# A graph kernel's sixteenth batch split in the hops: two of its tiles by dense products, two by gathered rows, 62 dense tiles in place of 64

## The reference

```
h = max(layernorm(x), 0)
x = x + typed_layer(h)            # gathers by source, sums by destination
h = max(layernorm(x), 0)
norm = deg_inv_sqrt[row] * deg_inv_sqrt[col]
out = h
for _ in range(2):                # the two hops
    h = segment_sum(h[row] * norm[:, None], col)
    out = out + h
x = x + out / 3
```

## Time and profile before

| | us |
|---|---|
| median of three runs | 3703.29 (3702.02 to 3703.51) |
| the profiled execution, its own time | 3704.01 |
| its span, first to last instruction | 3701.4 |
| PE busy | 3148.2 (85%) |
| ACT busy | 2655.3 (72%) |
| POOL busy | 2486.7 (67%) |
| DVE busy | 1789.1 (48%) |

### The profile page before, as it was taken

One profiled execution on the slowest core, in us unless ns is written; L12 is line 12 of the kernel. 1 busy time (PEld: TensorE's weight loads), 2 busy tenths in 40 slices (PEclk: granted clock), 3 DMA queues, 4 the chain that ended last, 5 costly groups with the idle time before them and its releaser, 6 DMA issues. The chain is left out here.

```text
span 3701.4 us, 64279 instructions
## 1 busy us (share of the span) xinstructions
PE 3148.2 (85%) x23900; PEld 2851.4 (77%) x23900; DVE 1789.1 (48%) x4166; ACT 2655.3 (72%) x2895; POOL 2486.7 (67%) x2635
## 2 busy tenths in 40 slices
PE   5658888897888866766667999999997999999998
PEld 2346777776777755544556999999997999999998
DVE  4665555455445568889884223332333222222223
ACT  3436666776667655445446889999996899999997
POOL 2467767777777767777775666666664766666666
PEclk8879989998999976677667999999998999999999
DMA  7453233433333275555556788888889778877876
GB/s 237 150 155 102 80 97 85 120 110 98 91 107 112 79 231 181 170 196 191 187 179 205 223 241 249 239 252 247 251 250 317 235 230 236 236 232 235 235 232 200
DMA packets 444208, 694.30 MB, mean 188 GB/s; under 512 B 62390, under 2 KB 373569, under 8 KB 435699
## 3 DMA queue, kind: packets, MB, share of 16 engines
q1 hardware_dynamic: 343827, 447.82, 37.6%
q0 software_dynamic: 99200, 241.92, 23.7%
q10 hardware_dynamic: 864, 0.39, 0.0%
HBM read 514.92 MB, written 174.97 MB: 186 GB/s over the span
## 5 line engine op out<-in xcount | busy, mean ns | idle before, releaser
L1122 POOL DMA_INDIRECT flat<-typed_table,index x1333 | 1299.7, 975 | 464.8 <-issue 400.2
L1289 ACT CAST strip_ring<-stage 128x1792 fp32r<-128x1792 uint8 x896 | 1495.3, 1688 | 147.3 <-PE wide L1492 125.5
L1492 PE MATMUL wide<-table_parts,strip_ring 128*128 128x256 f32 x12544 | 1543.0, 285 | 40.6 <-ACT strip_ring L1289 32.5
L1492 PEld LDWEIGHTS wide<-table_parts,strip_ring 128*128 128x128 f32 x12544 | 1528.3, 193 | 44.4 <-issue 26.3
L1122 POOL DMA_INDIRECT rows<-hop_table,index x1162 | 1111.5, 957 | 611.1 <-issue 313.8
L1271 ACT CAST stage<-wide 128x392 uint16<-128x392 f32 x1344 | 546.9, 516 | 519.6 <-PE wide L1403 519.5
L1403 PE MATMUL wide<-stage,flat 128*128 128x196 bf16 x2688 | 444.7, 284 | 296.5 <-DVE flat L1890 165.9
L1403 PEld LDWEIGHTS wide<-stage,flat 128*128 128x128 bf16 x2688 | 210.4, 107 | 513.3 <-DVE flat L1890 204.0
L1418 PE MATMUL turned_bank<-typed_ring,table_parts 128*128 128x256 f32 x3920 | 535.5, 296 | 77.2 <-ACT typed_ring L1282 70.4
L1835 DVE SCALAR_TENSOR_TENSOR sums<-sums_bank,in_upper,sums 128x128 f32 (+1 forms) x459 | 160.7, 350 | 871.9 <-PE sums_bank L1367 674.9
L1418 PEld LDWEIGHTS turned_bank<-typed_ring,table_parts 128*128 128x128 f32 x3920 | 506.2, 201 | 97.2 <-issue 58.6
(11 more groups left out here) (183 smaller groups left out, 1419.2 us busy)
## 6 DMA issues: line engine op xcount, KB each, us to landing
stage<-strips SPq DMA_DIRECT2D x896, 224.0 KB, 3.8
strips<-stage SPq DMA_DIRECT2D x64, 1568.0 KB
table_parts<-hop_table SPq DMA_DIRECT2D x28, 896.0 KB, 10.1
flat<-typed_table,index POOLq DMA_INDIRECT x1333
rows<-hop_table,index POOLq DMA_INDIRECT x1162
resid<-xin SPq DMA_DIRECT2D x50, 256.0 KB, 3.6
xin<-resid SPq DMA_DIRECT2D x50, 256.0 KB, 5.1
typed_table<-flat SPq DMA_DIRECT2D x49, 256.0 KB, 2.2
```

The lines of the kernel that those rows point to most:

```text
L1122: pool.indirect_dma_start(out=gathered(k, o % RING, c), out_offset=None, in_=tables[k], in_offset=bass.IndirectOffsetOnAxis(ap=index[:, ch ...
L1289: act.copy(strip_ring[:, number % STRIP_RING], counts_ring[place]).then_inc(strip_cast, 1)
L1492: last = pe.matmul(wide[:, nth % 4, 0:PARTS * P], strip_ring[:, number % STRIP_RING, b - first, :], table_parts[:, b, :, :].rearrange("p n ...
```

## The change

The hops now take 62 tiles by dense products. Of the sixteenth batch (number 15, `MIXED`) tiles 60 and 61 are dense, and tiles 62 and 63 come from gathered rows. A hop's gathered part begins at group 130 in place of 135: 78 groups in place of 73. The dense steps are spread over `hop_groups - 6` = 72 slots, so that six slots behind them have none where four had. Since the window moves on at the cut of batch 15 (slot 6 of a hop) and the batch is finished only in slot 74 or 75, a DVE copy puts the sums of the two gathered tiles aside (`later_part`, in a part of `index` that the hops no longer read). The strips of tiles 62 and 63 aren't built, stored or loaded.

```diff
--- before.py
+++ after.py
@@ -32,7 +32,9 @@
 COUNT_BASE = 256
 CELL_BANKS = 3
 DENSE_BATCHES = 16
-DENSE_TILES = DENSE_BATCHES * NODE_BLOCKS
+DENSE_TILES = 62
+MIXED = DENSE_BATCHES - 1
+MIXED_DENSE = DENSE_TILES - MIXED * NODE_BLOCKS
 PAIR_TILES = 9
 PARTS = 2
 STEP_BLOCKS = 14
@@ -41,7 +43,7 @@
 RELOAD_BLOCKS = 7
 RELOADS_AT_ONCE = 3
 STAGE_WORDS = 10320
-DENSE_SLOTS = 69
+SLOTS_BEHIND_DENSE = 6
 LEAD_TILES = 3
 LEAD_AT_ONCE = 3
 TYPED_BATCHES = 5
@@ -130,6 +132,7 @@
     dense_nodes = DENSE_TILES * P
     first_group = next(g for g in range(groups) if expected(g + 1) + MARGIN >= dense_nodes)
     hop_groups = groups - first_group
+    dense_slots = hop_groups - SLOTS_BEHIND_DENSE
     skipped = closed_before(first_group)
     assert skipped == DENSE_BATCHES - 1
     group_of_close = [next((g for g in range(groups - 1) if closed_before(g + 1) > s), groups - 1) for s in range(total)]
@@ -187,7 +190,7 @@
     def step_end(k, i):
 
         rest = steps_per_hop - lead_steps[k]
-        return lead_steps[k] + min(rest, -(-(i + 1) * rest // DENSE_SLOTS))
+        return lead_steps[k] + min(rest, -(-(i + 1) * rest // dense_slots))
 
     def slot_of_step(k, step):
         return next(i for i in range(hop_groups) if step_end(k, i) > step)
@@ -209,7 +212,7 @@
         return placed
 
     def hop_wanted(k):
-        dense = [(tile_slot[k][(s + 1) * NODE_BLOCKS - 1], s) for s in range(DENSE_BATCHES)]
+        dense = [(tile_slot[k][min((s + 1) * NODE_BLOCKS, DENSE_TILES) - 1], s) for s in range(DENSE_BATCHES)]
         return dense + [(slot, s) for slot, s in cuts[k] if s >= DENSE_BATCHES]
 
 
@@ -265,7 +268,7 @@
                 windows = skipped_in[k] + cut_before(k, g - first_groups[k]) - first_cut[k]
                 tops.append(windows * BATCH + (KEPT_TILES - 1) * P - 1)
             if g == first_groups[k]:
-                tops.append(dense_in[k] * BATCH - 1)
+                tops.append((dense_nodes if k else typed_nodes) - 1)
         top = min(tops)
         assert expected(g) + MARGIN <= top
         highest.append(top)
@@ -413,6 +416,8 @@
 
         counts_ring = [region(piece_words // 4, U8, start=table_words + STRIP_RING * piece_words + n * piece_words // 4)
                        .rearrange("p (b n) -> p b n", b=STEP_BLOCKS) for n in range(COUNT_RING)]
+        later_part = index[:, 0:(NODE_BLOCKS - MIXED_DENSE) * P].bitcast(F32).rearrange("p (b f) -> p b f", f=P)
+        assert (NODE_BLOCKS - MIXED_DENSE) * P <= first_group * CHUNKS
         new_parts = [region(NODE_BLOCKS * PARTS * P, F32R).rearrange("p (b n f) -> p b n f", b=NODE_BLOCKS, n=PARTS)
                      for _ in range(2)]
 
@@ -1733,8 +1738,15 @@
                     finish_done(dve.tensor_tensor(factors, batch_rstd[:, 1, 0:blocks], linked[:, 0:blocks], ALU.mult))
                     dve.wait_ge(fresh_ready, n + 1)
                 else:
-                    dve.tensor_tensor(in_blocks(values, blocks), source,
-                                      over_features(factors, blocks), ALU.mult).then_inc(fresh_made, 1)
+                    if not general and s == MIXED:
+                        dve.wait_ge(cut_made, next(first_cut[k] + j for j, (_, cut_batch) in enumerate(cuts[k]) if cut_batch == s) + 1)
+                        dve.tensor_tensor(in_blocks(values, blocks)[:, MIXED_DENSE:blocks], later_part,
+                                          over_features(factors[:, MIXED_DENSE:blocks], blocks - MIXED_DENSE), ALU.mult)
+                        blocks_in_source = MIXED_DENSE
+                    else:
+                        blocks_in_source = blocks
+                    dve.tensor_tensor(in_blocks(values, blocks)[:, 0:blocks_in_source], source[:, 0:blocks_in_source],
+                                      over_features(factors, blocks_in_source), ALU.mult).then_inc(fresh_made, 1)
                     dve.wait_ge(xin_in[xin_place[n]], xin_arrived(n))
                     dve.wait_ge(fresh_made, n + 1)
                 if k == HOPS:
@@ -1847,6 +1859,10 @@
 
                     kept, free = j % 2, (j + 1) % 2
                     dve.wait_ge(added, o + 1)
+                    if k and s == MIXED:
+                        if k > 1:
+                            dve.wait_ge(fresh_made, event_of[k - 1][MIXED] + 1)
+                        dve.tensor_copy(later_part, sums[:, kept, MIXED_DENSE:NODE_BLOCKS, 0:P])
                     if s == total - 1:
                         dve.memset(sums[:, free, :, :], 0.0).then_inc(cut_made, 1)
                         return
@@ -2052,7 +2068,7 @@
                             if k == 0:
                                 take_degrees(s, degrees_of(s) if is_dense(k, s) else batch_sums[:, :, P])
                             if is_dense(k, s):
-                                finish(n, k, s, in_blocks(own_in[:, s % 2, :]), ((k - 1) * DENSE_TILES + (s + 1) * NODE_BLOCKS) if k else 0, False)
+                                finish(n, k, s, in_blocks(own_in[:, s % 2, :]), ((k - 1) * DENSE_TILES + min((s + 1) * NODE_BLOCKS, DENSE_TILES)) if k else 0, False)
                             else:
                                 finish(n, k, s, batch_sums[:, :, 0:P], 0, False)
                 dve.nop()
```

## The result

| | before | changed |
|---|---|---|
| median, us | 3703.4 (3702.02 to 3705.77, 4 runs) | 3723.85 (3719.94 to 3726.81, 4 runs) |
| the profiled execution, us | 3704.01 | 3722.33 |
| its span, us | 3701.4 | 3720.6 |

The account below looks back on a forecast made before the run. PE was taken to bound the hops while they have dense steps, gathers the late first pass. Terms -8 - 1.9 - 4 - 2.5 - 0.1 = -16.5 us on 3704.0 gave 3687.5, median 3687 us; range 3671 to 3704.

Parts of the forecast that it names:

- The dense part: Each hop up to T, the end of its dense steps: 14 steps fewer, three groups' sums more, T 20.7 us sooner.
- The part behind T: After each hop's dense steps end (T), POOL sets the pace: last sums 20.6 us later in hop 2, 18.8 in hop 1.
- Stalls in hop 1: PE's 8.9 us of waits for ACT's casts in hop 1 about halve: -4 us, bounds 0 and -8.9.
- From hop 1 to hop 2: First lead step's cast wait shrinks, against possible slow clock: -2.5 us, bounds -3.7 and +1.5.
- Pass 0: First pass: 16 of 512 quads go, mostly hidden behind gathers; -8 us, bounds -28 and +8.
- Edits at nothing: In the hops, the new copy and one more scaling, 0.7 us a hop, are hidden; fewer strip loads, DMA traffic even.
- The slower one named: POOL falls behind in the hops; at 1.35 us a gather +27 us in all, 3714 us; chance 0.05.
- fewer waits of PE for ACT in hop 1: Sign expected in the changed profile: PE waits fewer times for ACT in hop 1; no size given.

Follow-up runs that it names:

- the chain cut: DVE finishes a batch ahead of reading the dense tiles that ended in the slot before: changed kernel 3683.57 us; same edit in the kernel before 3690.7 us.
- the run that made this part alone: Kernel before, strips 62 and 63 neither built nor stored, hops load strip 61 in their place: 3691.95 us, ratio 0.997.
- four slots behind T: Changed kernel, four slots after the dense steps, two last hop 1 tiles woven by piece: 3715.98 us; with DVE's tile reads behind the batch finish 3660.19 us.
- the kernel before with 67 slots: Kernel before, 64 dense tiles, dense steps spread over 67 slots in place of 69: 3754.36 us, ratio 1.0139.

## Why the prediction was wrong

The sum was -16.5 us, and the profiled execution came out at +18.3. By its own steps:

- **The dense part** (T sooner by 20.7 us in each hop). Right in hop 2, -22.1; slots of 11.01 and 9.33 us came as worked out. In hop 1 the part itself was right as well, and shows once the waits are gone: with the chain cut in both, dense 1 is 805.1 us with 64 tiles and 784.6 with 62, 20.5 less.
- **The part behind T** (the last sums at T + 30.7, 20.6 and 18.8 us later than before). Right: T + 31.2 and T + 31.3, later by 21.2 and 19.5. The rows of POOL that issue each 1.25 us and three buffers gave this within 0.7 us. In hop 1 the groups landed unevenly, but the last one when it should.
- **Stalls in hop 1** (-4 us, bounds 0 and -8.9). This is the step that failed. Dense 1 came out at +13.3 where -20.7 and -4 were forecast, an error of 38 us, which is more than the whole miss of 35. The failing sentence is "A slot of seven steps with a batch to cast gives ACT no room; the change has no slot of seven". It took a correlation for the cause, and a weak one: of the ten places of hop 1 in which the kernel before waits 0.5 or 2.13 us, three are in slots of seven steps and seven in slots of six. The right row was read, PE's waits for ACT, but not the next one up the chain: ACT in those places was waiting for DVE (26.6 us in 12 places), and not short of time. With that row the bound "0, they stay" could not have been the upper end. The waits depend on where a tile's last step falls in its slot, and the change from 430 / 69 = 6.2 steps a slot to 416 / 72 = 5.8 moved exactly that, from 0, 2 and 8 places with none, one and two steps behind to 5, 4 and 2. At 3.90, 2.13 and 0.5 us, that is 8 us before and 29 after, and the plan is enough to count it. The step then closes: -20.7 us of work, +18.5 us of waits and +15 us of slower matmuls (6,404 at 123.2 ns, 120.9 before) are +13, and +13.3 was measured.
- **The price of a stall.** Even with the right count the sum would have been short, since a stall was priced at its own length. The runs show 24.7 us of waits going together with 18.2 us of slower matmuls.
- **From hop 1 to hop 2** (-2.5 us, bounds -3.7 and +1.5). -0.3, within the bounds. The first lead step's cast waited 4.69 us where it had waited 3.72, so the longer tail gave DVE and ACT nothing: what they finish there depends on the last sums themselves. The clock cost nothing more, 12.00 us for the first 84 lead matmuls beside 11.85. The rule of the Trainium skill that was weighed there (Perfetto Trace Analysis, Matmul Optimizations: matmuls back to back, since the engine scales its power with its use) did not decide at the tail. It did where nobody had applied it, in the middle of hop 1: the windows above show the clock at 0.50 behind a wait of 3.90 us, and this trace agrees with the rule there.
- **Pass 0** (-8 us, bounds -28 and +8). Right in size: -12.4 in this profile, -8.5 over all profiles, -10.6 in the run that made this part alone. The way there is only partly the one named: POOL's waits for sums fell by 5.3 us, "seven or so" were expected, and the other part of the 12.4 was not traced. The longest wait did grow, from 8.0 to 10.1 us.
- **Edits at nothing.** Right: the kernel with the chain cut carries all of them.
- **The rivals.** The slower one named was POOL falling behind at 1.33 us a gather; POOL kept 1.25, and waited for PE in mid-hop to the end. The true way to slower was not among the rivals. A warning stood in the list of what would show it, fewer waits of PE for ACT in hop 1, and it came out the other way: 13 waits with 34.0 us.

The forecast's sum without its failed step, that is with +13.3 in place of -20.7 - 4 in hop 1, would be 3687.5 + 38.0 = 3725.5 us; 3722.3 was measured.

## What to carry to other kernels

When a change alters how many steps a slot holds, count on the new order of each engine, and not only on the bounding one, where an instruction that waits for the end of a slot stands ahead of one that the next slot needs; here three in-order engines in a ring turned such a place into a stop of 3.90 us. A wait named for a neighbour is to be followed to what the neighbour was waiting for before it gets a price or a cause. And a cheap exchange of two independent operations on an engine with time over (DVE is busy 48%) is worth trying before the tiling is changed: here it was worth 10 us in one kernel, 40 and 56 in two others.

## What the runs showed of the hardware

The granted clock does not fall in the wait alone but goes on behind it. Behind each of the five waits of 3.90 us in hop 1 of the changed kernel the slot's matmuls lost 1.6 to 2.5 us against full clock (12.74 us for 84 in place of 10.22 in the dearest), behind three of the four waits of 2.13 us 1.5 to 1.6, and behind the fourth and those of 0.5 us 0.1. A stall of PE of 3.90 us is therefore to be priced at some 1.5 times itself here. Over the whole of dense 1 the ratio was 1.7 in the changed kernel (25.7 us of idle time and 18.2 of clock), 1.5 with four slots behind T (39.9 and 21.5), and 1.4 in the kernel before with 67 slots (14.0 and 5).
